# A four-layer graph network: bias and row transfers re-queued, one scatter moved to the next block, the first embedding product moved, and one-hots of 128 rows in place of 35

## The chip, the core and the metric

The kernel runs on one core of a Trainium2 chip. The metric is the device time of one execution in microseconds; the time before is the median of three executions. The engines are called PE (TensorE, the matrix unit), DVE (VectorE), ACT (ScalarE), POOL (GpSimd) and SP (SyncE, which here only issues transfers).

## The reference

`x` holds 625 nodes of 768 features. Each of four stages is `x = x + layer(relu(layernorm(x)))`. What the layers compute, cut to the core:

```python
# L0: mean over the edges of each of 34 relations, one weight per relation
h1 = jnp.einsum('rni,rio->no', mean, W_rel) + x @ W_root + b_rgcn      # called "relations" below
out = gcn(h1, W_gcn) + b_gcn                                           # l0b
# L1: two gcn layers
h = relu(gcn(h, W1) + b1);  out = gcn(h, W2) + b2                      # l1a, l1b
# L2: the node's type embedding (3 types, 128 numbers) is joined to the features
h = jnp.concatenate([x, node_emb[node_type]], axis=-1)                 # 768 + 128 = 896
h = relu(rgcn_conv(h, ..., w_rel1, w_root1, b1))                       # l21, 3 kinds of edge, 896 -> 896
h = relu(rgcn_conv(h, ..., w_rel2, w_root2, b2))                       # l22
h = relu(rgcn_conv(h, ..., w_rel3, w_root3, b3))                       # l23
# L3: one gcn layer                                                    # l3
```

## The kernel before

The nodes lie in 5 tiles of 125 rows (`NP`, `NT`), the features in chunks of 128 (`fc` of them: 6 for width 768, 7 for 896). Float32 products are done as three products of rounded parts, hi by hi, hi by lo and lo by hi; ACT makes the high part of a chunk (`w_high`) and DVE subtracts it for the low part (`w_low`). The program has three parts that follow one another, with all engines meeting between them.

**The prepare block** (0 to 137.8 us). SP issues, in its queue's order: the edge lists, the ten pieces of `x`, a broadcast of the bias of the first layer into the DRAM tensor `sums` (L1309), the root weight `root_w` (L1310), a fill of spare rows (L1312) and, when the normalised rows are there, two stores of them to `rows` (L1316). PE turns the rows (L1668), ACT copies the turned chunks to `root_g` (L1400, L1401), and then PE takes turns of root products (L1684; `root(6)` first, which waits for `root_w`) and of slot counts (L1694), for which DVE builds comparison tables in five chunks (L1526 to L1533), two buffers deep, so that chunk 2 waits for the first `slots`. At the end the root products of node tiles 0 to 4 come from PE, ACT copies them into `h` (`take`), and POOL adds tile `d` to `sums` by an indirect DMA (L1367) for d = 0 to 3; the one of tile 4 is POOL's first transfer in the next block (L2100). These adds wait for the bias.

**`add_means`** (to 851.6 us). Thirty-three units of relation weights: POOL gathers rows of `rows` into `e_raw` (L2064), SP loads the list `list_now` and weights, ACT and DVE split them, PE multiplies, and POOL scatters the result onto `sums` (L2076). At its end ACT issues eight transfers that bring `sums` back to `h` in four parts of columns (`ROW_PARTS`, L2212); the next block's engines wait for each part by `loaded[i]`.

**`layers`** (from 854 us). All other layers, with one stream of weight chunks: SP loads chunk n into `w_raw`, a ring of 4 (L377), once DVE has taken chunk n - 4. Ahead of the first sums PE runs `AWAKE` times two products on nothing of use (L1019). The sums over edges are L821 and the products with weights L871; product tile k goes to one of two banks `ps_o`, and DVE's `take` (L602) adds it to `x`.

For `l21` the seventh chunk of the features is the embedding, and it is not stored per node: each node has a one-hot of its type, 35 columns wide (`HOT`: the three types at columns 0 to 2 and again at 32 to 34), and per kind of edge `typed_rows` (L843) multiplies the embedding with the seventh weight chunk into 35 rows, which ACT (L452) and DVE (L644, subtraction for the lower copy) put into `w_lo` as `typed`. Product tiles then have one pair of matmuls of 35 rows for this chunk in place of three pairs of 128. `w.order` of these weights begins with chunk 6, so it is loaded first. `turn` (L906) turns a tile of rows, the last chunk with 35 columns; ACT copies 750 columns (L477) and the 35 x 125 piece (L478).

## Time and profile before

| what | value |
|---|---|
| time, median of 3 runs | 1698.94 us (1697.83 to 1699.77) |
| the profiled execution | 1708.87 us, span 1707.2 us, granted clock 0.970 |
| PE / weight loads / DVE / ACT / POOL busy | 95% / 88% / 57% / 37% / 20% |
| data moved | 227.53 MB, 133 GB/s over the span |
| prepare block, last instruction of ACT ends | 137.8 us |
| relation weights end, ACT's last issue | 851.6 us |

The span is that of the instructions on the core; the profiled execution's time is 1.7 us more. The profiled execution is 9.9 us longer than the median of the runs without a profile. In the rows below a line is that of the kernel before, "[6.61 <-PE ...]" is the time that the engine sat idle before the row and what ended it, and "x34" counts instructions of one kind that the row stands for. PEclk is the clock that TensorE was granted, 1.00 being 2.4 GHz and 0.50 being 1.2 GHz.

### The profile page before, as it was taken

What the parts mean: (1) busy time and instruction counts of PE and PEld (TensorE: products, weight loads), DVE (VectorE), ACT (ScalarE), POOL (GpSimd) and SP (SyncE); (2) the same over time, 40 slices, a digit from 0 to 9 for tenths busy, and PEclk for the clock granted to TensorE, in tenths of its full rate; (3) what the DMA queues carried; (4) which work ended last, traced back from release to release, by engine and by line L of the source; (5) the groups of instructions that cost most, each with busy time, mean ns of one, the idle gap of its engine ahead of it and who ended that gap; (6) DMA issues with size and microseconds to landing.
All of it is one profiled execution on the core that took longest, in us unless ns stands there. A gap on an engine that the chain in (4) does not pass through costs nothing. (4 is left out here: it accounts for less than half of the span.)

```text
span 1707.2 us, 28150 instructions
## 1 busy us (share of the span) xinstructions
PE 1628.4 (95%) x9954; PEld 1498.6 (88%) x9955; DVE 981.2 (57%) x1486; ACT 626.3 (37%) x858; POOL 333.3 (20%) x297
## 2 busy tenths in 40 slices
PE   6998998999999999999799989999999999999997
PEld 4766887999999998888699988899899999999997
DVE  7784885786766678555376573255252442523372
ACT  6113564555555565555143223112231222312230
POOL 1203544453443343442110000000010000000000
PEclk8869999999999999999899999999999999999999
DMA  6225897687997799996442130231122112221101
GB/s 221 44 69 139 243 261 196 190 253 206 253 263 202 203 270 247 266 263 173 74 122 65 52 114 24 72 92 36 56 66 84 56 57 83 58 73 56 56 28 46
DMA packets 96605, 227.53 MB, mean 133 GB/s; under 512 B 11987, under 2 KB 36326, under 8 KB 96524
## 3 DMA queue, kind: packets, MB, share of 16 engines
q1 hardware_dynamic: 68471, 150.07, 27.6%
q0 software_dynamic: 21552, 71.98, 18.7%
q10 hardware_dynamic: 6501, 4.33, 1.0%
q8 instruction: 60, 0.98, 0.2%
q14 instruction: 21, 0.17, 0.0%
HBM read 186.94 MB, written 41.29 MB: 134 GB/s over the span
## 5 line engine op out<-in xcount | busy, mean ns | idle before, releaser
L871 PE MATMUL layers_ps_o<-layers_w_lo,layers_g_hi 128*125 128x384 f32 (+2 forms) x900 | 239.4, 347 | 4.6 <-DVE layers_w_lo L644 4.6
L2513 PE MATMUL l_means_ps<-l_means_w_hi,l_means_g_hi 128*128 128x512 f32 (+1 forms) x912 | 238.3, 342 | 3.6 <-DVE l_means_g_lo L2373 3.6
L2147 ACT CAST l_means_w_hi<-w_raw 128x768 fp32r<-128x768 f32 x204 | 170.2, 838 | 190.2 <-PE l_means_ps L2513 186.7
L2362 DVE TENSOR_TENSOR l_means_w_lo<-w_raw,l_means_w_hi 128x768 fp32r<-128x768 f32 x204 | 186.6, 948 | 89.2 <-ACT l_means_w_hi L2147 89.0
L2513 PE MATMUL l_means_ps<-l_means_w_hi,l_means_g_lo 128*128 128x512 f32 (+1 forms) x912 | 235.5, 339 | 0.0
L2513 PE MATMUL l_means_ps<-l_means_w_lo,l_means_g_hi 128*128 128x512 f32 (+1 forms) x912 | 234.0, 338 | 0.0
L871 PE MATMUL layers_ps_o<-layers_w_hi,layers_g_hi 128*125 128x384 f32 (+1 forms) x870 | 230.5, 346 | 0.8 <-DVE layers_w_lo L584 0.8
L871 PE MATMUL layers_ps_o<-layers_w_hi,layers_g_lo 128*125 128x384 f32 (+1 forms) x870 | 228.6, 344 | 0.0
L2497 PE MATMUL l_means_ps<-pick,e_hi 128*128 128x256 f32 (+1 forms) x612 | 167.7, 304 | 18.8 <-issue 18.3
L655 DVE TENSOR_TENSOR h_lo<-layers_ps_o,h_hi 125x768 fp32r<-125x768 f32 (+1 forms) x45 | 45.1, 1002 | 237.8 <-ACT h_hi L484 237.8
L871 PEld LDWEIGHTS layers_ps_o<-layers_w_lo,layers_g_hi 128*125 128x125 f32 (+1 forms) x900 | 162.7, 186 | 12.4 <-DVE layers_w_lo L644 4.9
L2513 PEld LDWEIGHTS l_means_ps<-l_means_w_hi,l_means_g_hi 128*128 128x128 f32 x912 | 152.5, 189 | 22.7 <-issue 2.9
L2513 PEld LDWEIGHTS l_means_ps<-l_means_w_lo,l_means_g_hi 128*128 128x128 f32 x912 | 153.8, 189 | 20.9
L2513 PEld LDWEIGHTS l_means_ps<-l_means_w_hi,l_means_g_lo 128*128 128x128 f32 x912 | 154.1, 188 | 19.1
L2076 POOL DMA_INDIRECT sums<-l_means_y,l_means_row_now x76 | 129.2, 1700 | 206.7 <-ACT l_means_y L2182 176.9
L2497 PE MATMUL l_means_ps<-pick,e_lo 128*128 128x256 f32 (+1 forms) x612 | 165.6, 300 | 0.0
L871 PEld LDWEIGHTS layers_ps_o<-layers_w_hi,layers_g_hi 128*125 128x125 f32 x870 | 156.5, 186 | 8.5 <-issue 3.4
L871 PEld LDWEIGHTS layers_ps_o<-layers_w_hi,layers_g_lo 128*125 128x125 f32 x870 | 158.2, 186 | 3.5
L2373 DVE TENSOR_TENSOR l_means_g_lo<-l_means_ps,l_means_g_hi 128x512 fp32r<-128x512 f32 (+1 forms) x126 | 78.3, 637 | 125.8 <-ACT l_means_g_hi L2161 124.8
L821 PE MATMUL layers_ps_g<-a,h_hi 125*128 125x316 f32 x590 | 136.0, 312 | 7.1 <-DVE h_lo L626 2.5
L2497 PEld LDWEIGHTS l_means_ps<-pick,e_hi 128*128 128x128 f32 x612 | 119.7, 196 | 22.1 <-issue 19.8
L2064 POOL DMA_INDIRECT e_raw<-rows,l_means_src_now x99 | 127.0, 1283 | 49.5 <-POOL l_means_src_now L2061 27.2
(363 smaller groups left out, 2405.6 us busy)
## 6 DMA issues: line engine op xcount, KB each, us to landing
w_raw<-in_L_gnn_W_rel SPq DMA_DIRECT2D x204, 384.0 KB, 6.8
layers_w_raw<-in_L_gnn_w_rel SPq DMA_DIRECT2D x39, 384.0 KB, 7.8
layers_w_raw<-in_L_gnn_w_rel SPq DMA_DIRECT2D x21, 448.0 KB, 8.3
layers_a_raw<-adj SPq DMA_DIRECT2D x9, 769.0 KB
layers_w_raw<-in_L_gnn_W SPq DMA_DIRECT2D x18, 384.0 KB, 3.5
list_now<-targets SPq DMA_DIRECT2D x33, 192.0 KB
layers_w_raw<-in_L_gnn_w_root SPq DMA_DIRECT2D x13, 384.0 KB, 3.4
layers_w_raw<-in_L_gnn_w_root SPq DMA_DIRECT2D x7, 448.0 KB, 4.5
```

Of the source, the lines that this page charges most:

```text
L655: v.tensor_tensor(in_halves(h_lo[:, k, 0:layer.width]), out_rows(bank, layer.width), in_halves(h_hi[:, k, 0:layer.width]).bitcast(F32), AL ...
L821: mm = t.matmul(to[:, at:at + PART[p]], rows[:, k, f * 128:(f + 1) * 128], a[:, k, cols], start=(k == 0 and i == 0), stop=(k == NT - 1 and ...
L871: mm = t.matmul(ps_o[0:NP, i % 2, a_half, 0:half], g, part_of_w[:, a_half * half:(a_half + 1) * half], start=(f == order[0] and n == 0), s ...
L2064: nc.gpsimd.indirect_dma_start(out=e_raw[:, j, :], out_offset=None, in_=rows, in_offset=bass.IndirectOffsetOnAxis(ap=src_now[:, j:j + 1], ...
L2076: nc.gpsimd.indirect_dma_start(out=sums, in_=y[:, j, :], in_offset=None, compute_op=ALU.add, out_offset=bass.IndirectOffsetOnAxis(ap=row_n ...
L2147: nc.scalar.copy(w_hi[:, f, :], w_raw[:, f, :]).then_inc(w_hi_ready, 1)
L2362: v.tensor_tensor(w_lo[:, f, :], w_raw[:, f, :], w_hi[:, f, :].bitcast(F32), ALU.subtract)\
L2373: v.tensor_tensor(g_lo[:, f:f + per, at], sums_in_bank(f // per, tiles), g_hi[:, f:f + per, at].bitcast(F32), ALU.subtract).then_inc(g_rea ...
L2497: mm = t.matmul(sums, e[:, j, f * 128:(f + 1) * 128], pick[:, j, 0:cols], start=(j == 0 and part == 0), stop=(j == UNIT - 1 and part == 1))
L2513: mm = t.matmul(ps_y[j][:, o0:o1], g[:, f, at], w[:, f, o0:o1], start=(f == 0 and opens and g is g_hi and w is w_hi), stop=(f == fc - 1 an ...
```

## The change

- SP issues the bias broadcast behind the two stores of rows, so `root_w` follows `x` at once. `WARM_ROWS`, a count of products without use ahead of the turns, goes from 16 to 32.
- The scatter of root tile 3 leaves the prepare block and is issued by POOL in the next one, ahead of that of tile 4.
- Of the eight transfers that bring `sums` back, ACT issues two (part 0) before the blocks meet, and SP six at the start of the last block, ahead of the bias and of the first weights. `AWAKE` goes from 8 to 6.
- `typed_rows` of the first kind of `l21` moves on PE from ahead of that layer to behind product tile 0 of `l1b`. ACT and DVE split chunk 6 of its weight, and build `typed`, correspondingly earlier. The other two kinds stay.
- The one-hots are 128 columns wide (zeros from column 35), so that the pair of matmuls of the embedding has 128 rows; the turned chunk is copied together with the other six.

The diff, cut to what the prediction speaks of:

```diff
+def fetch_rows(engine, source, h, i, loaded):
+    at = slice(ROW_PARTS[i][0] * 128, ROW_PARTS[i][1] * 128)
+    rows = source.rearrange("(k p) f -> p k f", p=NP)
+    for part in (slice(0, 112), slice(112, NP)):
+        engine.dma_start(h[part, :, at], rows[part, :, at]).then_inc(loaded[i], 16)
...
+    @block.sync
+    def _(sp):
+        for i in range(1, len(ROW_PARTS)):
+            fetch_rows(sp, source, h, i, loaded)
...
-AWAKE = 8
+AWAKE = 6
...
-            nc.scalar.copy(tile_columns(g_hi, k, fc - 1), turned_tile(k, fc - 1)).then_inc(layer.g_hi_ready, 1)
-            nc.scalar.copy(g_hi[0:HOT, fc - 1, column(k):column(k) + NP], ps_g[0:HOT, k % 2, (fc - 1) * 128:(fc - 1) * 128 + NP])\
-                .then_inc(layer.g_hi_ready, 1)
+            nc.scalar.copy(tile_columns(g_hi, k, fc), turned_tile(k, fc)).then_inc(layer.g_hi_ready, 1)
...
         summed_high(l1b)
+        w_high(l21.w[0], 0)
+        typed_rows_high(l21.w[0])
         root_of(l1b, 0)
...
+        dve.wait_ge(emb_high, 1)
+        v.tensor_tensor(emb_parts[1], part[:, 0:HOT], emb_parts[0].bitcast(F32), ALU.subtract).then_inc(emb_ready, 1)
         summed_low(l1b)
+        w_low(l21.w[0], 0)
         add_bias(l1b)
...
             take(l1b, k)
+            if k == 1:
+                typed_rows_low(l21.w[0])
...
-                    terms = ((g_hi[0:HOT, f, at], typed),)
+                    terms = ((g_hi[:, f, at], w_lo[:, f, :]),)
...
-        gcn_products(l1b, range(NT - 1))
+        gcn_products(l1b, (0,))
+        pe.wait_ge(emb_ready, 1)
+        typed_rows(l21.w[0])
+        gcn_products(l1b, range(1, NT - 1))
+        pe.wait_ge(typed_ready, 1)
         turn(0)
...
-            sp.dma_start(sums, bias.unsqueeze(0).broadcast_to([N, width])).then_inc(bias_stored, 16)
             sp.dma_start(root_w[:], w_root.rearrange("(f p) o -> p f o", p=128)).then_inc(root_loaded, 16)
...
+            sp.dma_start(sums, bias.unsqueeze(0).broadcast_to([N, width])).then_inc(bias_stored, 16)
             sp.wait_ge(nodes_used, tiles // group)
...
-            for d in range(NT - 1):
+            for d in range(NT - 2):
...
+            for d in (NT - 2, NT - 1):
+                nc.gpsimd.indirect_dma_start(out=sums, in_=second.h[:, d, 0:width], in_offset=None, compute_op=ALU.add,
+                                             out_offset=bass.IndirectOffsetOnAxis(ap=node_rows[:, d:d + 1], axis=0))\
+                    .then_inc(root_added, 16)
```

What the change does to the order of instructions is shown at three places. First SP's queue in the prepare block, before, from the last two pieces of `x` to the first relation weights:

```order
L1308 DMA x_rows<-in_x 112x768
L1308 DMA x_rows<-in_x 13x768
L1309 DMA sums<-in_L_gnn_b_rgcn 625x768
L1310 DMA prep_root_w<-in_L_gnn_W_root 128x6x768
L1312 DMA sums<-prep_empty_rows 2304x1x128
L1316 DMA rows<-h_rows 112x5x768
L1316 DMA rows<-h_rows 13x5x768
L1319 DMA w_raw<-in_L_gnn_W_rel 128x768 x6
```

The same place of the change:

```order
L1327 DMA x_rows<-in_x 112x768
L1327 DMA x_rows<-in_x 13x768
L1328 DMA prep_root_w<-in_L_gnn_W_root 128x6x768
L1330 DMA sums<-prep_empty_rows 2304x1x128
L1334 DMA rows<-h_rows 112x5x768
L1334 DMA rows<-h_rows 13x5x768
L1335 DMA sums<-in_L_gnn_b_rgcn 625x768
L1338 DMA w_raw<-in_L_gnn_W_rel 128x768 x6
```

The bias broadcast moved past three transfers and now stands last ahead of the relation weights.

Second DVE at the start of `l1b`'s products, before: the last pair of splits of `l1b` (w_lo, g_lo), the bias for five tiles, and the takes of tiles 0 and 1:

```order
L584 TENSOR_TENSOR layers_w_lo<-layers_w_raw,layers_w_hi 128x768
L591 TENSOR_TENSOR layers_g_lo<-layers_ps_g,layers_g_hi 128x630
L597 TENSOR_TENSOR x_rows<-x_rows,layers_bias_rows 125x768 x5
L602 SCALAR_TENSOR_TENSOR x_rows<-layers_ps_o,dinv,x_rows 125x768
L88 BN_STATS layers_stats<-x_rows 125x6 x2
L602 SCALAR_TENSOR_TENSOR x_rows<-layers_ps_o,dinv,x_rows 125x768
L88 BN_STATS layers_stats<-x_rows 125x6 x2
```

And of the change (L601 is the old L584, L614 the old L597, L619 the old L602):

```order
L601 TENSOR_TENSOR layers_w_lo<-layers_w_raw,layers_w_hi 128x768
L608 TENSOR_TENSOR layers_g_lo<-layers_ps_g,layers_g_hi 128x630
L601 TENSOR_TENSOR layers_w_lo<-layers_w_raw,layers_w_hi 128x896
L614 TENSOR_TENSOR x_rows<-x_rows,layers_bias_rows 125x768 x5
L619 SCALAR_TENSOR_TENSOR x_rows<-layers_ps_o,dinv,x_rows 125x768
L88 BN_STATS layers_stats<-x_rows 125x6 x2
L619 SCALAR_TENSOR_TENSOR x_rows<-layers_ps_o,dinv,x_rows 125x768
L661 TENSOR_TENSOR layers_w_lo<-layers_ps_g,layers_w_lo 3x896
L88 BN_STATS layers_stats<-x_rows 125x6 x2
```

The split of `l21`'s first weight chunk (128x896) came ahead of the bias and of every take, and the subtraction for `typed` behind the take of tile 1.

Third PE at the end of `l1b`'s last product tile, before: the three pairs of `typed_rows` (L843), and the first pair of `l21`:

```order
L871 MATMUL layers_ps_o<-layers_w_hi,layers_g_hi 125x384 x2
L871 MATMUL layers_ps_o<-layers_w_lo,layers_g_hi 125x384 x2
L871 MATMUL layers_ps_o<-layers_w_hi,layers_g_lo 125x384 x2
L843 MATMUL layers_ps_g<-layers_w_hi,layers_g_lo 35x448 x2
L843 MATMUL layers_ps_g<-layers_w_lo,layers_g_lo 35x448 x2
L843 MATMUL layers_ps_g<-layers_w_hi,layers_g_lo 35x448 x2
L871 MATMUL layers_ps_o<-layers_w_hi,layers_g_hi 125x448 x2
```

And of the change, where they stand now, between product tiles 0 and 1 of `l1b` (L863 is the old L843, L891 the old L871):

```order
L891 MATMUL layers_ps_o<-layers_w_hi,layers_g_hi 125x384 x2
L891 MATMUL layers_ps_o<-layers_w_lo,layers_g_hi 125x384 x2
L891 MATMUL layers_ps_o<-layers_w_hi,layers_g_lo 125x384 x2
L863 MATMUL layers_ps_g<-layers_w_hi,layers_g_lo 35x448 x2
L863 MATMUL layers_ps_g<-layers_w_lo,layers_g_lo 35x448 x2
L863 MATMUL layers_ps_g<-layers_w_hi,layers_g_lo 35x448 x2
L891 MATMUL layers_ps_o<-layers_w_hi,layers_g_hi 125x384 x2
```

The three pairs moved ahead of four of the five product tiles of `l1b`.

## Rows read from the trace of the kernel before

**Rows 1.** The page: busy time of TensorE, its share and count

```profile
PE 1628.4 (95%) x9954; PEld 1498.6 (88%) x9955; DVE 981.2 (57%) x1486; ACT 626.3 (37%) x858; POOL 333.3 (20%) x297
```

**Rows 2.** Timeline of PE, 27 to 66 us (start, duration, operation, idle before)

```profile
27.12 1.40 PE L1668 MATMUL prep_ps<-ident,h_rows 125*128 125x125 f32 x10 [0.21 <-ACT prep_root_g L1401]
34.40 6.89 PE L1684 MATMUL prep_ps<-prep_root_w,prep_root_g 128*125 128x384 f32 x12 [5.88 <-DMA prep_root_w<-in_L_gnn_W_root]
41.13 2.91 PE L1694 MATMUL prep_ps<-prep_is_tile,w_raw 125*128 125x186 f16 x34
...
65.29 4.06 PE L1684 MATMUL prep_ps<-prep_root_w,prep_root_g 128*125 128x384 f32 x12
```

**Rows 3.** Timeline of DVE in the prepare block: tables of chunk 2; index build

```profile
44.08 1.29 DVE L1526 TENSOR_TENSOR prep_is_slot<-prep_iota,prep_slot_of 125x2176 f16<-125x2176 f16 x1 [6.61 <-PE prep_ps L1694]
...
65.49 0.35 DVE L1547 TENSOR_SCALAR s_src_index<-prep_ps 128x186 int32<-128x186 f32 x1 [4.74 <-PE prep_ps L1694]
```

**Rows 4.** Timeline of ACT in the prepare block, its last turned copy

```profile
29.03 0.27 ACT L1401 COPY prep_root_g<-prep_ps 128x125 f32<-128x125 f32 x1
```

**Rows 5.** Table by stretches: engines' busy time, PEclk, DMA share, GB/s

```profile
16.00:20.00 4.00, 2.46 (x12) 0.91 (x10) 3.31 (x12) 2.69 (x7) 0.00 (x0) 1.00 0.95 346
27.00:35.00 8.00, 2.00 (x11) 1.54 (x12) 7.89 (x7) 5.12 (x8) 0.00 (x0) 0.89 0.34 123
141.00:143.00 2.00, 0.00 (x0) 0.00 (x0) 0.00 (x0) 0.59 (x1) 0.00 (x0) 0.85 0.00 0
979.00:986.00 7.00, 7.00 (x42) 7.00 (x41) 5.99 (x8) 0.00 (x0) 0.00 (x0) 1.00 0.99 250
```

**Rows 6.** Timeline of ACT at the two block changes; last, of POOL's root scatters

```profile
142.41 1.28 ACT L2139 ACT_TABLE_LOAD   x1 [4.60 <-PEq L64]
...
847.79 3.83 ACTq L2212 DMA_DIRECT2D h_rows<-sums  x8
854.13 0.72 ACT L134 CAST a<-adj_all 125x630 fp32r<-125x630 uint16 x1 [15.71 <-PEq L64]
...
130.36 1.99 POOL L1367 DMA_INDIRECT sums<-h_rows,node_rows  x1 [29.55 <-ACT h_rows L1409]
...
DMA to landing us min/median/max: 10.0/10.6/13.9
```

**Rows 7.** Timeline of ACT and DVE in the first unit of relation weights

```profile
158.87 0.84 ACT L2143 CAST e_hi<-e_raw 128x768 fp32r<-128x768 f32 x1 [0.15 <-DMA e_raw<-rows,l_means_src_now]
...
159.97 1.07 DVE L2351 TENSOR_SCALAR pick<-list_now,s_slot_dst 128x384 fp32r<-128x384 f32 x3 [5.55 <-DMA list_now<-targets]
```

**Rows 8.** Timeline of ACT; then the page's list of DMA issues (landing)

```profile
865.45 0.84 ACT L448 CAST layers_w_hi<-layers_w_raw 128x768 fp32r<-128x768 f32 x1
...
layers_w_raw<-in_L_gnn_W_gcn SPq DMA_DIRECT2D x6, 384.0 KB, 10.7
```

**Rows 9.** Timeline of DVE, ACT and PE, 978 to 1037 us

```profile
978.53 4.42 DVE L597 TENSOR_TENSOR x_rows<-x_rows,layers_bias_rows 125x768 f32<-125x768 f32 x5
983.52 1.02 DVE L602 SCALAR_TENSOR_TENSOR x_rows<-layers_ps_o,dinv,x_rows 125x768 f32<-125x768 f32 x1 [0.56 <-PE layers_ps_o L871]
...
1013.26 0.94 ACT L448 CAST layers_w_hi<-layers_w_raw 128x896 fp32r<-128x896 f32 x1 [3.76 <-DMA layers_w_raw<-in_L_gnn_w_rel]
...
1025.08 1.10 PE L871 MATMUL layers_ps_o<-layers_w_lo,layers_g_hi 35*125 35x448 f32 x2 [4.56 <-DVE layers_w_lo L644]
...
1036.16 0.67 PE L871 MATMUL layers_ps_o<-layers_w_lo,layers_g_hi 35*125 35x448 f32 x2
```

**Rows 10.** Timeline of PE in kind 1; then its groups by form

```profile
1146.60 0.57 PE L871 MATMUL layers_ps_o<-layers_w_hi,layers_g_hi 128*125 128x448 f32 x2
...
1148.22 0.56 PE L871 MATMUL layers_ps_o<-layers_w_lo,layers_g_hi 128*125 128x448 f32 x2
...
1150.23 0.56 PE L871 MATMUL layers_ps_o<-layers_w_lo,layers_g_hi 128*125 128x448 f32 x2
...
L871 PE MATMUL layers_ps_o<-layers_w_lo,layers_g_hi 35*125 35x448 f32 x30 | 10.5, 430 | 4.6 <-DVE layers_w_lo L644 4.6
```

More of the change, by code:

```diff
@@ L102, in row_scales, with load_rows @@
     newton_rsqrt(v, then, rstd[:, at], var[:, at], tmp[:, at])
-def load_rows(nc, block, sem, loaded, h, parts, dinv, adj_all, a, a_parts, a_ready, buffers):
+ROW_PARTS = ((0, 1), (1, 2), (2, 4), (4, 6))
+def fetch_rows(engine, source, h, i, loaded):
[3 more added lines that the diff above has]
+        engine.dma_start(h[part, :, at], rows[part, :, at]).then_inc(loaded[i], 16)
+def load_rows(nc, block, sem, source, loaded, h, parts, dinv, adj_all, a, a_parts, a_ready, buffers):
     fc = ROW_PARTS[-1][-1]
@@ L500, in kind_step @@
             w = after(layer.w[r])
-            if layer is l21:
+            if layer is l21 and r > 0:
                 typed_rows_high(layer.w[r])
@@ L553, in _ @@
         root_of(l1b, 2)
-        for f in range(l21.w[0].fc):
+        for f in range(1, l21.w[0].fc):
             w_high(l21.w[0], f)
@@ L646, in turned_low @@
         def turned_low(layer, k):
-            dve.wait_ge(layer.g_hi_ready, 2 * k + 2)
+            dve.wait_ge(layer.g_hi_ready, k + 1)
             fc = layer.w[0].fc - 1
@@ L687, in kind_products @@
         def kind_products(layer, r):
-            if layer is l21:
+            if layer is l21 and r > 0:
                 typed_rows_low(layer.w[r])
@@ L767, in _ @@
             if k == NT - 1:
-                dve.wait_ge(emb_high, 1)
-                v.tensor_tensor(emb_parts[1], part[:, 0:HOT], emb_parts[0].bitcast(F32), ALU.subtract).then_inc(emb_ready, 1)
                 turned_low(l21, 1)
-                for f in range(l21.w[0].fc):
+                for f in range(1, l21.w[0].fc):
                     w_low(l21.w[0], f)
             take(l1b, k)
+            if k == 1:
+                typed_rows_low(l21.w[0])
             then(row_statistics(v, stats, x, k))
@@ L904, in turn @@
             for f in range(l21.w[0].fc):
-                size = HOT if f == l21.w[0].fc - 1 else 128
-                mm = t.transpose(ps_g[0:size, k % 2, f * 128:f * 128 + NP], h[:, k, f * 128:f * 128 + size], ident[0:NP, 0:NP])
+                mm = t.transpose(ps_g[:, k % 2, f * 128:f * 128 + NP], h[:, k, f * 128:(f + 1) * 128], ident[0:NP, 0:NP])
             mm.then_inc(l21.turned, 1)
         def kind_products(layer, r):
-            if layer is l21:
-                if r == 0:
-                    pe.wait_ge(emb_ready, 1)
-                    pe.wait_ge(layer.g_ready, 1)
-                else:
-                    pe.wait_ge(layer.e_taken, place_of(layer, r, 0) - 1)
+            if layer is l21 and r > 0:
+                pe.wait_ge(layer.e_taken, place_of(layer, r, 0) - 1)
                 typed_rows(layer.w[r])
@@ L962, in root_columns @@
                     if by_type and f == w.fc - 1:
-                        terms = ((typed[:, out_chunk], g_hi[0:HOT, f, :]),)
+                        terms = ((w_lo[:, f, out_chunk], g_hi[:, f, :]),)
                     else:
@@ L1066 @@
 WARM = 16
-WARM_ROWS = 16
+WARM_ROWS = 32
 def by_runs(rows, run):
@@ L1815 @@
 Background = namedtuple("Background", "src dst etype kinds adj adj_all ident h node_types emb rows_loaded")
-ROW_PARTS = ((0, 1), (1, 2), (2, 4), (4, 6))
 def add_means(nc, tag, units, w_rel, rows, sums, plan, src_index, slot_dst, row_index, row_inv, targets, node_rows, list_rows,
@@ L2099, in _ @@
             nc.gpsimd.nop().then_inc(index_ready, 1)
-            nc.gpsimd.indirect_dma_start(out=sums, in_=second.h[:, NT - 1, 0:width], in_offset=None, compute_op=ALU.add,
-                                         out_offset=bass.IndirectOffsetOnAxis(ap=node_rows[:, NT - 1:NT], axis=0))\
-                .then_inc(root_added, 16)
+            for d in (NT - 2, NT - 1):
+                nc.gpsimd.indirect_dma_start(out=sums, in_=second.h[:, d, 0:width], in_offset=None, compute_op=ALU.add,
+                                             out_offset=bass.IndirectOffsetOnAxis(ap=node_rows[:, d:d + 1], axis=0))\
+                    .then_inc(root_added, 16)
             iota(key_iota[:], [[1, keys]])
@@ L2207, in _ @@
             act.wait_ge(all_added, 1)
-            to = second.h
-            summed_rows = sums[0:N, :].rearrange("(k p) f -> p k f", p=NP)
-            for i, (f0, f1) in enumerate(ROW_PARTS):
-                for part in (slice(0, 112), slice(112, NP)):
-                    nc.scalar.dma_start(to[part, :, f0 * 128:f1 * 128], summed_rows[part, :, f0 * 128:f1 * 128])\
-                        .then_inc(second.rows_loaded[i], 16)
+            fetch_rows(nc.scalar, sums[0:N, :], second.h, 0, second.rows_loaded)
         @block.vector
@@ L2299, in embeddings @@
                 then(ins)
-                then(v.memset(second.h[:, :, width:width + HOT], 0.0))
+                then(v.memset(second.h[:, :, width:width + 128], 0.0))
                 for at in (0, 32):
@@ L2605, in gnn_kernel @@
         a_parts = sem("a_parts")
-        loaded = load_rows(nc, block, sem, rows_loaded, h, parts, dinv, adj_all, a, a_parts, a_ready, buffers)
+        loaded = load_rows(nc, block, sem, sums0[0:N, :], rows_loaded, h, parts, dinv, adj_all, a, a_parts, a_ready, buffers)
         layers(nc, block, sem, buffers, loaded, x, h, acc, parts, a, a_parts, a_ready, adj_all, adj2, inv_dram, dinv, ident, d, out)
```

## Prediction

> **What bounds the kernel now.** I read the page first: TensorE is busy 95% of the span and no other engine over 57% [rows 1], so time can only go where PE idles, runs at the lower clock, or does work that it could do faster. Next I took PE's timeline and looked for "idle before" over 0.3 us, and for the same operation with two durations. Four places lie under this change. In the prepare block PE idles 5.88 us until `root_w` has landed, and its first twelve root products then take 6.73 us (34.40 to 41.13) where twelve take 4.06 later [rows 2]; DVE, whose table for chunk 2 waits for the slots behind these products, idles 6.61 us with them [rows 3]. At the change of blocks ACT idles 4.60 us the first time, and the second time from the end of its issues (847.79 + 3.83 = 851.62) to 854.13, 2.51 us [rows 6]. In `l21` PE waits 4.56 us for `typed` [rows 9]. And in each product tile of `l21` the pair of matmuls with 35 rows stands in a wider gap than the others [rows 10].
>
> **Bias behind the rows.** Before, the bias broadcast goes ahead of `root_w`. The reader should see that from 27 to 35 us, while PE waits, the transfer engines are only 34% busy and move 123 GB/s, where 16 to 20 us show 95% and 346 GB/s [rows 5]: what runs there is slow, not queued behind much else. Without it `root_w` (2304 KB) takes 2304/346 = 6.8 us once `x` is through. Lower bound of its landing: `x` is in by about 10 us, hence 17 us. Upper: only the slow stretch goes, 34.4 - 8 = 26.4 us. Both are ahead of the last turned copy of ACT, which ends at 29.03 + 0.27 = 29.30 [rows 4], and on which the same products wait. So they start at 29.3, 5.1 us earlier. The doubled warm-up products should leave the clock at 2.4 GHz, so the twelve take 4.0 us, not 6.73; slots of chunk 0 then stand at 33.3 and not at 41.13, and end 2.8 us later at 36.1. From there DVE decides: it is free at 44.08 - 6.61 = 37.47 [rows 3] and needs about 5.57 us for each of chunks 2 to 4 (an even beat that PE's rounds follow), so the last table is there at 54.2 and the last slots end at 57.2, where before the next root products began at 65.29 [rows 2]. Term: **-8.0**. If the clock stays low for the twelve, slots 0 end at 38.8, chunk 2 starts 5.3 earlier, and the term is -5.3. Behind this point everything waits for PE: DVE's index build sat idle 4.74 us for the last slots [rows 3]. The bias itself lands by about 45 us, ahead of the first scatter-add; its cover is some 18 us, and gone it would cost what it exceeds.
>
> **Root tile 3 moved.** Its scatter is issued at 130.36 and the median of its kind lands 10.6 us later, at 141.0 [rows 6]; from 141 to 143 us nothing moves [rows 5], and ACT goes on at 142.41, 1.4 us behind the landing. The second block change, with no scatter of that kind at its end, takes 2.5 us, not 4.6. I read this as the blocks meeting only when that transfer is done: **-2.1**; if they don't wait for it, 0. In the next block POOL issues one scatter more ahead of the three gathers of the first unit, 1.99 us and 0.3 between [rows 6]. The gathers' last split on ACT ends at 158.87 + 0.84 = 159.71, but DVE, held by `list_now` until 159.97, needs the third split only after three `pick` (1.0) and two `e_lo` (1.8), at about 162.8 [rows 7]. The cover is 3.0 us and hides the 2.3: **0**.
>
> **Rows brought back.** ACT issues 2 transfers, not 8, so its 3.83 us become 1.0 and the last block begins 2.9 us sooner [rows 6]. But the six others now are SP's, 0.48 us each and ahead of bias and weights, so `W_gcn` is asked for at the same moment as before, about 854.4. It landed 10.7 us later, at 865.1, and ACT took it at 865.45 [rows 8]: a slack of 0.35. The early start is thus lost on the weight. If the landing does not move, the term is -0.35; if the 2.9 us by which the rows' transfers shift go wholly onto it, it is 865.1 + 2.9 - 865.45 = +2.6. It has the rows' traffic right ahead of it now, so I take the middle: **+1.0**. Six `AWAKE` rounds for eight save nothing, since PE waits for rows behind them.
>
> **First embedding product.** Gains: the wait for `typed` of 4.56 us [rows 9]. Behind it PE works at the lower clock: the 35-row pair there takes 1.10 us and the same pair a tile later 0.67; in that proportion over the pair, the turn and the next three pairs it is 2.3 us. ACT waited 3.76 us at 1013.26 for the fifth weight chunk, whose place in the ring comes free only when chunk 0 is split; with that split some 20 us earlier this wait goes; PE, whose 18 pairs ahead of the 1025.08 row need 7.3 us at 0.405, had about 1.6 of it. Together -8.4. Cost: the products need weight chunk 6, which is asked for behind a transfer of edge counts. From 979 to 986 the transfer engines are 99% busy at 250 GB/s [rows 5], 448 KB taking 1.8 us; the chunk lands between 981 and 986, and I take 985, since four chunks share that stretch. High part 0.94, a low part hardly longer and the hand-overs give 987.1. PE ends tile 0 at 983.5, as the take of tile 0 shows [rows 9], so it stalls 3.6 us, and the clock falls as above but with nothing but full pairs behind, 1.3 us; hand-over of `typed` 0.5. Behind that wait on DVE stand the bias adds (982.95 - 978.53 = 4.42) and the takes: take 0 ends at 992.5, while PE wants its bank for tile 2 only at 994, so no second stall. Term: -8.4 + 5.4 = **-3.0**; -8.0 if the chunk lands by 981.4, and 0 if at 988.
>
> **128 rows.** Four starts of pairs without a 35-row one span 1148.22 - 1146.60 = 1.62 us, and four with one 1150.23 - 1148.22 = 2.01 [rows 10], so such a pair costs 0.39 more than one of 128 rows. There are 15 (x30 in pairs), and one in each of the 7 chunks of the root product: 22 x 0.39 = 8.6. Three of them lie where PE waits anyway: **-7.4**; bounds 0 and -8.6. The one copy of 875 columns for 750 and 125, the wider zeros and the wider turn stand beside PE's products, 0.
>
> The row says that 35 rows are slower. The Trainium skill, "TensorE: Matmul & The Clock Gate", section "Why this matters for your kernels", has a single matmul of 32 rows take the same time as one of 128. By that rule this term would be 0 and the sum -12.1; the trace does not agree, with 2.01 for 1.62 us, unless the gap comes from something else that stays.
>
> **Sum**: -8.0 - 2.1 + 1.0 - 3.0 - 7.4 = -19.5. The profiled execution takes 1708.9 us, so 1689.4 with a profile; it stands 9.9 us above the median of the plain runs, and the same off that median, 1698.9 - 19.5, gives **1679.5 us**.
>
> **Rivals.**
> - *The first weight chunk of `l21` is early*, by 981.4: the stall in `l1b` is gone, 1674.5. For it, the engines are free for other queues while the counts load; against, 99% busy until 986. 0.12.
> - *Rows in a matmul cost nothing* and the gap has another cause (the change doesn't do what it says there): 1679.5 + 7.4 = 1686.9. 0.09.
> - *Two scatters hold up the gathers.* Landings of this kind run from 10.0 to 13.9 us [rows 6], the longer ones where two follow closely. If the gathers come 3.9 us later beside the 2.3, 6.2 - 3.0 = +3.2: 1682.7; with twice that delay 1686.6. 0.14.
> - *Weights late at both waits*: `W_gcn` by the whole 2.9 (+1.6 on my term) and chunk 6 at 988 (+3): 1684.1. 0.11.
> - *Slower than before*: the stall ahead of the embedding product costs PE its clock for long. `l1b`'s four tiles behind it have 18 pairs each, 0.35 us apart, 25 us in all, and take twice that at 1.2 GHz. It outweighs the other terms and the 0.2% once the clock is down for some 22 us. Against: behind 4.56 us of idleness the pair times are normal again within 5 us, after 5.88 us within about 7 [rows 2, 9]. At worst 1679.5 + 25 = 1704. 0.02.
>
> **How the numbers follow.** My forecast, 1675.5 to 1683.5 with the bounds of single terms, has 0.52. The range takes in the early chunk in part, the rule of rows and the scatters: 1673 to 1687. A difference under 0.2% (3.4 us) can't be told from none here; faster than that means under 1695.5, which all cases but the last reach: faster 0.96, within 0.02, slower 0.02.
>
> **What the new profile should show.** The first L1684 row at about 29.3 without a wait for `root_w`, and the last slots ending near 57. ACT's idle time at the first block change near 2.5 us, and e_hi not waited for by DVE. ACT's first high part of `W_gcn` at about 856.3 (865.45 less 10.1, plus 1.0), waiting for the transfer. A PE row at the embedding product with 3 to 4 us of idleness, and none for `typed` in `l21`. Pairs of the seventh chunk 0.405 us apart like the rest. I am wrong if DVE's table of chunk 2 starts later than 39, if the gathers of the first unit make PE wait, or if PE idles more than 5 us behind tile 0 of `l1b`.

## The result

The change makes the kernel 0.5% faster: the ratio of its time to that of before is 0.9947, with a 95% interval of 0.9928 to 0.9967 (nine runs each, medians 1692.14 and 1703.21 us). On the 1698.94 us shown ahead of the prediction that is about 9 us, to 1689.9; the forecast was 19.5, and 1689.9 lies above both of its ranges (to 1683.5, and to 1687 with the rivals). The two profiled executions differ by 8.6 us in their span (1707.2 and 1698.6).

The page of the changed kernel; TensorE is as busy as before, to be read with [rows 1], and a DMA that brings rows back now stands in the chain that ended last:

```profile
PE 1621.6 (95%) x9966; PEld 1499.9 (88%) x9967; DVE 981.5 (58%) x1486; ACT 625.3 (37%) x853; POOL 334.7 (20%) x297
...
PE 42%; DVE 5%; DMA 2%; ACT 1%; issue 0%; SPq 0%; DVEq 0%
PE layers_ps_o L891 25%; PE layers_ps_g L841 9%; PE layers_ps_g L985 4%; PE layers_ps_g L1017 3%; DMA layers_w_raw<-in_L_gnn_w_rel 1%; DVE layers_w_lo L601 1%; DMA h_rows<-sums 1%; DVE h_lo L643 0%; DVE layers_stats L88 0%; ACT h_hi L488 0%; ACT layers_w_hi L465 0%; DVE x_rows L619 0%; DVE layers_part L688 0%; PE layers_ps_g L863 0%; DMA layers_w_raw<-in_L_gnn_w_root 0%
```

A single total does not say which part did what, because one stretch of the kernel takes a different time in each trace. So I divide each trace at instructions that all kernels have, and give the time from one of these cuts to the next. All cuts are starts of rows of the timelines of ACT and DVE, but for the end of ACT's last take.

| from ... to ... | before | after | difference | forecast |
|---|---|---|---|---|
| start to the end of ACT's last take of the prepare block | 137.81 | 129.32 | -8.49 | -8.0 |
| to ACT's first instruction of `add_means` | 4.60 | 1.15 | -3.45 | -2.1 |
| to the first low part of 512 columns in the first unit | 33.11 | 35.19 | +2.08 | 0 |
| to ACT's first transfer of rows (32 units) | 672.27 | 673.82 | +1.55 | 0 |
| to ACT's first instruction of the last block | 6.34 | 6.34 | 0 | -2.9 |
| to the first high part of `W_gcn` | 11.32 | 17.27 | +5.95 | +3.9 |
| to `l0b`'s take of tile 0 | 18.15 | 20.45 | +2.30 | 0 |
| to `l1b`'s take of tile 0 | 99.92 | 109.42 | +9.50 | } -3.0 |
| to the low part of `l21`'s second product | 54.29 | 44.89 | -9.40 | } |
| to the last take | 660.66 | 652.04 | -8.62 | -7.4 |

The differences sum to -8.58. The gain of the prepare block is lost almost to the microsecond at the second change of blocks (+8.25 in three rows), where +1.0 was forecast.

PE in the prepare block, to be read with [rows 2]: no wait for `root_w` is left, the twelve root products start at 28.67 and take 4.11 us (6.89 before), and the last ones start at 57.17 where they started at 65.29.

```profile
28.67 4.11 PE L1703 MATMUL prep_ps<-prep_root_w,prep_root_g 128*125 128x384 f32 x12 [0.92 <-ACT prep_root_g L1420]
32.61 2.91 PE L1713 MATMUL prep_ps<-prep_is_tile,w_raw 125*128 125x186 f16 x34
...
57.17 4.06 PE L1703 MATMUL prep_ps<-prep_root_w,prep_root_g 128*125 128x384 f32 x12
```

ACT at the two block changes, to be read with [rows 6]: the first idle time is 1.15 us, not 4.60. At the second, the issues take 1.21 us and not 3.83, but the time from their start to the next block (845.82 - 839.48) is 6.34 us, exactly as before (854.13 - 847.79).

```profile
130.47 1.28 ACT L2158 ACT_TABLE_LOAD   x1 [1.15 <-PEq L64]
...
839.48 1.21 ACTq L114 DMA_DIRECT2D h_rows<-sums  x2
845.82 0.72 ACT L151 CAST a<-adj_all 125x630 fp32r<-125x630 uint16 x1 [16.49 <-PEq L64]
...
863.09 0.83 ACT L465 CAST layers_w_hi<-layers_w_raw 128x768 fp32r<-128x768 f32 x1
```

DVE in the last block: before, its row multiplications (L158) waited for no transfer, as in these two rows of the kernel before:

```profile
856.58 0.83 DVE L158 TENSOR_TENSOR h_rows<-h_rows,dinv 125x640 f32<-125x640 f32 x1
...
859.62 0.82 DVE L158 TENSOR_TENSOR h_rows<-h_rows,dinv 125x640 f32<-125x640 f32 x1
```

Now (L175) they wait three times, 7.45 us in all. The weight `W_gcn` is not waited for in this trace: ACT's row at 863.09 above has no idle time before it.

```profile
849.33 0.83 DVE L175 TENSOR_TENSOR h_rows<-h_rows,dinv 125x640 f32<-125x640 f32 x1 [2.66 <-DMA h_rows<-sums]
...
853.70 0.83 DVE L175 TENSOR_TENSOR h_rows<-h_rows,dinv 125x640 f32<-125x640 f32 x1 [2.81 <-DMA h_rows<-sums]
...
858.72 0.82 DVE L175 TENSOR_TENSOR h_rows<-h_rows,dinv 125x640 f32<-125x640 f32 x1 [1.98 <-DMA h_rows<-sums]
```

And around the moved embedding product, to be read with [rows 9]: ACT gets the weight chunk at 986.52, PE has waited 5.35 us for its low part, its pairs are then 0.73 to 0.75 us apart, and the take of tile 0, at 983.52 before, is at 992.96.

```profile
986.52 0.94 ACT L465 CAST layers_w_hi<-layers_w_raw 128x896 fp32r<-128x896 f32 x1 [8.78 <-DMA layers_w_raw<-in_L_gnn_w_rel]
...
988.72 0.93 PE L863 MATMUL layers_ps_g<-layers_w_hi,layers_g_lo 128*35 128x448 f32 x2 [5.35 <-DVE layers_w_lo L601]
989.45 0.95 PE L863 MATMUL layers_ps_g<-layers_w_lo,layers_g_lo 128*35 128x448 f32 x2
...
992.96 1.02 DVE L619 SCALAR_TENSOR_TENSOR x_rows<-layers_ps_o,dinv,x_rows 125x768 f32<-125x768 f32 x1
```

### The profile page after: what moved, and what is told of

It reads as the page before. It is cut to its first block, busy times and chain, and to the rows that moved or that the text cites. A ratio compares the mean times of both kernels' runs of the same rounds, so it can differ in the third digit from the quotient of the medians.

```text
span 1698.6 us, 28171 instructions
## 1 busy us (share of the span) xinstructions
PE 1621.6 (95%) x9966; PEld 1499.9 (88%) x9967; DVE 981.5 (58%) x1486; ACT 625.3 (37%) x853; POOL 334.7 (20%) x297
## 4 chain that ended last, share of the span: by engine, by line
PE 42%; DVE 5%; DMA 2%; ACT 1%; issue 0%; SPq 0%; DVEq 0%
PE layers_ps_o L891 25%; PE layers_ps_g L841 9%; PE layers_ps_g L985 4%; PE layers_ps_g L1017 3%; DMA layers_w_raw<-in_L_gnn_w_rel 1%; DVE layers_w_lo L601 1%; DMA h_rows<-sums 1%; DVE h_lo L643 0%; DVE layers_stats L88 0%; ACT h_hi L488 0%; ACT layers_w_hi L465 0%; DVE x_rows L619 0%; DVE layers_part L688 0%; PE layers_ps_g L863 0%; DMA layers_w_raw<-in_L_gnn_w_root 0%
## 5 line engine op out<-in xcount | busy, mean ns | idle before, releaser
L891 PE MATMUL layers_ps_o<-layers_w_lo,layers_g_hi 128*125 128x384 f32 (+1 forms) x900 | 237.6, 345 | 0.0
L891 PE MATMUL layers_ps_o<-layers_w_hi,layers_g_hi 128*125 128x384 f32 (+1 forms) x870 | 229.7, 345 | 0.8 <-DVE layers_w_lo L601 0.7
L891 PE MATMUL layers_ps_o<-layers_w_hi,layers_g_lo 128*125 128x384 f32 (+1 forms) x870 | 228.6, 344 | 0.0
L891 PEld LDWEIGHTS layers_ps_o<-layers_w_lo,layers_g_hi 128*125 128x125 f32 x900 | 163.9, 186 | 3.9
L891 PEld LDWEIGHTS layers_ps_o<-layers_w_hi,layers_g_hi 128*125 128x125 f32 x870 | 157.4, 186 | 6.1 <-DVE layers_w_lo L601 1.4
L891 PEld LDWEIGHTS layers_ps_o<-layers_w_hi,layers_g_lo 128*125 128x125 f32 x870 | 158.2, 186 | 3.4
```

What stands on the lines that cost most here:

```text
L891: mm = t.matmul(ps_o[0:NP, i % 2, a_half, 0:half], g, part_of_w[:, a_half * half:(a_half + 1) * half], start=(f == order[0] and n == 0), s ...
```

## The experiments

**Each part alone.** First the row fetch, alone on the kernel before (`AWAKE` goes with it):

```diff
+        for i in range(1, len(ROW_PARTS)):
+            fetch_rows(sp, source, h, i, loaded)
...
-            for i, (f0, f1) in enumerate(ROW_PARTS):
+            fetch_rows(nc.scalar, sums[0:N, :], second.h, 0, second.rows_loaded)
```

> The kernel before with the row fetch alone changed. Theory: the last block does not start sooner when ACT issues two transfers in place of eight, because in both traces it starts 6.34 us after ACT's first issue; parts 1 to 3 are therefore only asked for at its start, DVE waits for them and PE's clock falls: the first high part of W_gcn comes about 6 us later against ACT's first issue, and the take of tile 0 of l0b about 8 us later (891.8 for 883.6), so about 8 us slower in all. Rival (the term of my prediction): the block starts 2.9 us sooner and only the weight's landing costs, +1.0 us in all.

Measured: ratio 1.0068 (1.0042 to 1.0094), slower. From ACT's first transfer to the block 6.34 us; to the first high part of `W_gcn` 16.74 us for 11.32; from there to the take 18.16, as before. So +5.4 us in the trace and +8.25 in that of the changed kernel. The mechanism stands: the block does not start sooner, and the rival's -2.9 is not there.

The plain runs lose more than this stretch of the trace: 0.42 to 0.94% are 7 to 16 us. The profiled execution, 1705.8 us, is the fastest of the ten; the granted clock of the ten is 0.967 on the mean, that of the kernel before 0.971. Where the rest is lost was not traced. The effect of `AWAKE` was not tested apart.

Of the 2.8 us between the two traces, 0.5 lie ahead of the high part of `W_gcn` (17.27 and 16.74), and 2.3 behind it. These 2.3 are a matter of TensorE's clock, which two groups of rows show. PE's first sum behind the wait for DVE in this kernel:

```profile
864.94 0.55 PE L838 MATMUL layers_ps_g<-a,h_hi 125*128 125x316 f32 x2 [2.37 <-DVE layers_g_lo L608]
865.33 0.46 PE L838 MATMUL layers_ps_g<-a,h_lo 125*128 125x316 f32 x2
865.62 0.47 PE L838 MATMUL layers_ps_g<-a,h_hi 125*128 125x316 f32 x2
```

and in the changed kernel:

```profile
865.69 0.89 PE L841 MATMUL layers_ps_g<-a,h_hi 125*128 125x316 f32 x2 [4.26 <-DVE layers_g_lo L608]
866.38 0.73 PE L841 MATMUL layers_ps_g<-a,h_lo 125*128 125x316 f32 x2
866.90 0.73 PE L841 MATMUL layers_ps_g<-a,h_hi 125*128 125x316 f32 x2
```

After 2.37 us of idleness the pairs behind the first are 0.29 us apart, at 2.4 GHz; after 4.26 us they are 0.52 to 0.53 apart, at 1.2 GHz, for 5 us, and ten steps, each 0.15 to 0.30 us longer, make the 2.3. The table of stretches has the granted clock of both from 866 to 870 us, first the changed kernel, then the other:

```profile
866.00:870.00 4.00, 4.00 (x16) 4.00 (x16) 3.68 (x5) 1.87 (x3) 0.00 (x0) 0.50 0.75 204
```

```profile
866.00:870.00 4.00, 4.00 (x29) 4.00 (x28) 4.00 (x6) 2.54 (x4) 0.00 (x0) 1.00 0.81 225
```

Then the one-hots of 128 rows alone:

```diff
-                    terms = ((g_hi[0:HOT, f, at], typed),)
+                    terms = ((g_hi[:, f, at], w_lo[:, f, :]),)
```

> The kernel before with one-hots of 128 rows alone. Theory: the pair of matmuls with 35 rows costs 0.39 us more than one with 128, 22 times, so -8.6 us, all of it between the third tile of l21's first kind and the end of l22's start; everything ahead of l21 stays within 0.1 us. Rival (row count does not matter, the gap is something else): 0, and what the changed kernel gained there comes from the moved embedding product (-8.6 then shows only together with it).

Measured: from `l0b`'s first take to the last take 806.34 us, 814.87 before: -8.5 us, in the place expected. Over all traces that stretch is at 815.1 us on the mean in the six kernels that have the old one-hots and the old place of the embedding product (814.28 to 816.04), and `row_sizes` below, with 128 and 96 rows, has 806.33 too: -8.7. The ratio, 0.9974 (0.9945 to 1.0003), says less than this (below). The rival is out.

The first embedding product alone:

```diff
-        gcn_products(l1b, range(NT - 1))
+        gcn_products(l1b, (0,))
+        pe.wait_ge(emb_ready, 1)
+        typed_rows(l21.w[0])
+        gcn_products(l1b, range(1, NT - 1))
```

> The kernel before with the first embedding product alone moved. Theory: PE stalls 5.2 to 5.4 us behind tile 0 of l1b for the weight chunk that lands at about 986.5, the clock falls, take 0 is 9.4 us later, and by the second tile of l21 all of it is given back by the wait for the typed rows that is gone: 0.0 to +0.2 us in all. Rival (my prediction): -3.0 us, since the ring of weight chunks runs ahead.

Measured: ratio 1.0001 (0.9974 to 1.0027). From `l0b`'s first take to `l1b`'s 109.47 us for 99.92, and from there to `l21`'s second product 44.27 for 54.29: -0.5 in all, which is 0 within the 2 us by which this stretch varies. So it is as the theory said, and not -3.0.

The bias behind the rows alone, with 32 warm-up products:

```diff
-            sp.dma_start(sums, bias.unsqueeze(0).broadcast_to([N, width])).then_inc(bias_stored, 16)
...
+            sp.dma_start(sums, bias.unsqueeze(0).broadcast_to([N, width])).then_inc(bias_stored, 16)
-WARM_ROWS = 16
+WARM_ROWS = 32
```

> The kernel before with the bias broadcast behind the rows and 32 warm-up products, nothing else. Theory: ACT's last take of the prepare block ends 8.5 us sooner, and as the rest of the kernel waits for nothing that is bound to the clock on the wall, the whole kernel is 8 us shorter. Rival: the scatter of root tile 3, still in this block, keeps its distance to the last take, so the gain stays, but the first unit's gathers or the relation loop lose part of it again: 4 to 6 us.

Measured: ACT's last take ends at 129.90 us, 7.9 sooner than in the trace of before. Over all traces of this study it is at 136.6 on the mean with the old prepare block (nine kernels, 135.64 to 137.81) and at 129.8 with the new one (four, 129.32 to 130.14), so the edit is worth 6.8 us, and the trace of before was a late one. The ratio is 0.9980 (0.9956 to 1.0004), about half of what the stage gained, and can't tell theory from rival. Which of the two edits did it, the order of the transfers or the 32 products, was not tested apart. Why the ratios are blurred can be seen in the traces: the 32 units of relation weights (fourth row of the table) took 661.3 to 674.3 us over the thirteen kernels, one trace each, all with the same instructions in that loop; the four traces of one and the same chip have 661.3, 664.5, 671.4 and 674.3. A part worth 8 us is within that spread. Each of the other stretches repeats within about 2.2 us among the kernels that have the same code there, and those from ACT's first transfer of rows to `l1b`'s take within 0.1, but for one of 0.3.

The scatter of root tile 3 alone:

```diff
-            for d in range(NT - 1):
+            for d in range(NT - 2):
...
+            for d in (NT - 2, NT - 1):
```

> The kernel before with the scatter of root tile 3 alone moved. Theory: the change of blocks takes 1.2 us in place of 4.6 to 4.8, and the first unit takes 1.5 to 2 us longer from its first instruction to the first low part of its second stage (35.2 for 33.1 to 33.5), since its list of targets and the gathers come later: -1.5 to -2 us together. Rival: the first unit keeps its 33.3 us, and the whole 3.5 stays.

Measured, in the one execution of this kernel: 1.15 us at the change of blocks and 35.63 us in the first unit. The nine kernels without this edit have 4.44 to 4.80 there (mean 4.64) and 33.11 to 34.90 (mean 33.77), so it is -3.5 and +1.9: -1.6 us together. What the 4.6 us were is settled by the landing of the scatter of root tile 3: in each of the nine kernels ACT goes on 1.47 us behind it (before: issued at 130.36, landed 10.58 us later at 140.94, ACT at 142.41), though the landing itself moves from 133.2 to 140.9 us. In the changed kernel the loss can be seen on DVE and ACT, to be read with [rows 7]:

```profile
150.57 1.08 DVE L2365 TENSOR_SCALAR pick<-list_now,s_slot_dst 128x384 fp32r<-128x384 f32 x3 [8.72 <-DMA list_now<-targets]
```

```profile
150.90 0.84 ACT L2162 CAST e_hi<-e_raw 128x768 fp32r<-128x768 f32 x1 [1.83 <-DMA e_raw<-rows,l_means_src_now]
```

DVE waits 8.72 us for the list, 5.55 before, and ACT 1.83 for the third gather, 0.15 before. Counted from the start of the block, the third gather's split starts 4.0 us later than before (20.4 for 16.5). The third split ends at 151.74, before DVE wants it at about 153.4; the list, a plain transfer of SP's, came 20.1 us after the start of the block and not 17.6, and DVE's rows put it ahead of the gathers in setting the time. Had the list been on time, the gathers would have cost about 0.9 us (an estimate: DVE would have wanted the third split at 150.8, 2.5 us sooner). Why it is later beside one scatter more is open.

**The change without the row fetch.** If the account holds, taking back one of five parts must nearly double the gain.

```diff
-            fetch_rows(nc.scalar, sums[0:N, :], second.h, 0, second.rows_loaded)
+            for i, (f0, f1) in enumerate(ROW_PARTS):
-AWAKE = 6
+AWAKE = 8
```

> The changed kernel with the row fetch and AWAKE put back to what they were. Theory (the row fetch lost 8.25 us of 17.7 gained): from ACT's first row issue to the take of tile 0 of l0b 29.5 us, as before, not 37.7; the whole kernel about 8 us faster than the change and 17 faster than before, ratio 0.990. Rival (what the first block gains is lost behind the second change of blocks in any case, for instance on the weights of l0b): that stretch stays above 33 us and the ratio near 0.994.

Measured: ratio 0.9902 (0.9869 to 0.9934), median 1684.34 us. ACT's rows, to be read with those of the change above:

```profile
837.91 3.83 ACTq L2215 DMA_DIRECT2D h_rows<-sums  x8
844.25 0.72 ACT L134 CAST a<-adj_all 125x630 fp32r<-125x630 uint16 x1 [15.75 <-PEq L64]
...
855.57 0.83 ACT L448 CAST layers_w_hi<-layers_w_raw 128x768 fp32r<-128x768 f32 x1
```

ACT is at its issues for 3.83 us, the block starts 6.34 us after the first of them, as in the other kernels, and the high part of `W_gcn` comes 11.32 us later; the take of `l0b` stands 35.82 us behind the first transfer, 44.06 in the changed kernel. (The 29.5 and 37.7 of the expectation are counted from the start of the block and not from the first transfer, 6.34 us less: 29.48 measured.) The rival is out: the gain of the first block is not lost here in any case.

**The embedding product one tile later**, on top of that:

```diff
-        gcn_products(l1b, (0,))
+        gcn_products(l1b, (0, 1))
...
-        w_low(l21.w[0], 0)
         add_bias(l1b)
...
-            if k == 1:
+            if k == 2:
                 typed_rows_low(l21.w[0])
             then(row_statistics(v, stats, x, k))
+            if k == 0:
+                w_low(l21.w[0], 0)
```

> As the run without the row fetch, and the first embedding product one tile later: on PE behind product tile 1 of l1b, on DVE the split of the weight behind the statistics of tile 0 and that of the typed rows behind the take of tile 2. Theory: chunk 6 lands at 986.5 and PE is busy with tile 1 until 989.9, so PE does not stall and the clock stays up; from l0b's first take to l1b's first 99.9 us, not 109.4, and in all 6 to 8 us faster than the run beside it, ratio to before 0.986. Rival: the time goes into the wait for the later weight chunks of l21 instead (three waits on ACT for their landing), and at the second product tile of l21 less than 2 us are left of it.

Measured: ratio 0.9858 (0.9829 to 0.9888), median 1677.51 us, the fastest kernel of this study. PE around the product shows neither a wait nor the lower clock:

```profile
982.84 0.51 PE L875 MATMUL layers_ps_o<-layers_w_hi,layers_g_lo 128*125 128x384 f32 x2
983.19 0.57 PE L847 MATMUL layers_ps_g<-layers_w_hi,layers_g_lo 128*35 128x448 f32 x2
...
984.41 0.51 PE L875 MATMUL layers_ps_o<-layers_w_hi,layers_g_hi 128*125 128x384 f32 x2
```

From `l0b`'s first take to `l21`'s second product it takes 147.03 us; in the changed kernel it is 154.31, in the run beside it 154.99, and in the two kernels with the same one-hots and the product in its old place (`onehots_only`, `row_sizes`) 153.63 and 153.25. So the move is worth 6 to 7 us when PE does not have to wait for it, and nothing here, where it waited 5.35 us and went on at the lower clock.

**Which row counts cost.** The pair of matmuls of the embedding with 128, 64 and 96 rows:

```diff
-                    terms = ((g_hi[:, f, at], w_lo[:, f, :]),)
+                    rows = (128, 64, 96, 128)[typed_number(w)]
+                    terms = ((g_hi[0:rows, f, at], w_lo[0:rows, f, :]),)
```

> The kernel before with one-hots of 128 rows, but the pair of matmuls of the embedding with 128 rows in l21's first kind, 64 in the second and 96 in the third (the rows left out are zeros). Theory (a change of the number of row groups that a matmul uses costs): the pair of 64 and that of 96 cost about 0.39 us more than one of 128, as 35 did. Rival (only a number of rows that is not a multiple of 32 costs): 64 and 96 cost nothing more. Second rival (the cost grows with the rows missing): 64 costs more than 96, and both less than 0.39.

Measured, in the groups by form (count, busy, mean ns of one):

```profile
L870 PE MATMUL layers_ps_o<-layers_w_lo,layers_g_hi 96*125 96x448 f32 x10 | 2.9, 369 | 0.0
```

The mean of 369 ns is that of the full pairs (the pairs of 35 rows had 430, [rows 10]), and the pairs are 0.41 us apart like their neighbours: 96 rows cost as much as 128. The number 64 had gone to the root weights, which use another line, so no kind ran with it; hence a second kernel with `(128, 128, 64, 65)`:

> As row_sizes, where 96 rows cost nothing (pairs 0.41 us apart as their neighbours) and the 64 fell on no kind: now 64 rows in the second kind and 65 in the third. Theory formed from that run: a matmul of at most 64 rows, coming between matmuls of 125 or 128, costs the 0.39 us per pair, one of more than 64 nothing; 64 shows 1.21 to 1.23 us for the two pairs behind the one ahead in place of 0.8, 65 shows none. Rival: only 32 rows or partial row groups cost, so both 64 and 65 cost nothing, or 65 costs and 64 does not.

Measured:

```profile
L870 PE MATMUL layers_ps_o<-layers_w_lo,layers_g_hi 64*125 64x448 f32 x10 | 3.4, 414 | 0.0
L870 PE MATMUL layers_ps_o<-layers_w_lo,layers_g_hi 65*125 65x448 f32 x10 | 2.9, 369 | 0.0
L870 PEld LDWEIGHTS layers_ps_o<-layers_w_lo,layers_g_hi 64*125 64x125 f32 x10 | 1.4, 182 | 1.4 <-issue 1.4
L870 PEld LDWEIGHTS layers_ps_o<-layers_w_lo,layers_g_hi 65*125 65x125 f32 x10 | 1.8, 187 | 0.1
```

And a pair of 64 rows among its neighbours:

```profile
1136.83 0.56 PE L870 MATMUL layers_ps_o<-layers_w_hi,layers_g_lo 128*125 128x448 f32 x2
1137.32 0.67 PE L870 MATMUL layers_ps_o<-layers_w_lo,layers_g_hi 64*125 64x448 f32 x2
1137.92 0.68 PE L870 MATMUL layers_ps_o<-layers_w_hi,layers_g_hi 128*125 128x448 f32 x2
1138.43 0.56 PE L870 MATMUL layers_ps_o<-layers_w_lo,layers_g_hi 128*125 128x448 f32 x2
```

From 1136.83 to 1138.43 these are 1.60 us where three steps of full pairs take 1.21; a pair of 65 at 1201.44 has its neighbours at 1201.04, 1201.85 and 1202.26, 1.22 us. So of the five numbers tried, 35 and 64 rows cost 0.39 us a pair, and 65, 96 and 128 nothing more; the step lies between 64 and 65. Numbers between 35 and 64, or below 35, were not run. From `l0b`'s first take to the last take this kernel has 810.09 us, 3.8 more than with 96 and 128 rows; its five pairs of 64 account for 2.0, and the rest is within what the stretch varies by. The weight loads show where the time lies: ahead of the ten loads of 64 rows the engine stood idle 1.4 us, ahead of those of 65 rows 0.1. That a load of few rows can't be made beside a running matmul of many would explain it; it is a guess, not shown.

**What starts the last block.** Two kernels, one execution each. POOL's part, on the kernel before; the memsets write a buffer that is read no more:

```diff
             nc.gpsimd.nop().then_inc(all_added, 1)
+            for j in range(3):
+                nc.gpsimd.memset(y[:, j, :], 0.0)
```

> The kernel before with three memsets of 128 x 768 on POOL behind the instruction that releases ACT's row fetch (they write a buffer that nothing reads any more). Six of six kernels start the last block 6.34 us after ACT's first row issue, with two or with eight issues. Theory: POOL sets that time, so the block starts later by the whole duration of the three memsets. Rival: another engine or a fixed time sets it, and it stays 6.34.

Measured, on POOL and ACT:

```profile
836.88 2.09 POOL L2137 MEMSET l_means_y<- 128x768 f32 x3 [5.51 <-DMA sums<-l_means_y,l_means_row_now]
...
836.80 3.83 ACTq L2214 DMA_DIRECT2D h_rows<-sums  x8
845.29 0.72 ACT L134 CAST a<-adj_all 125x630 fp32r<-125x630 uint16 x1 [18.28 <-PEq L64]
```

The memsets take 2.09 us, and the block starts 8.49 us after ACT's first transfer, 2.15 later than in the other kernels. Then ACT's part, sixteen transfers of half the columns for eight:

```diff
+                    for half in range(2):
+                        cols = slice((f0 + f1) * 64 - (1 - half) * (f1 - f0) * 64, (f0 + f1) * 64 + half * (f1 - f0) * 64)
+                        nc.scalar.dma_start(to[part, :, cols], summed_rows[part, :, cols])\
```

> The kernel before with the eight row transfers of ACT cut into sixteen of half the columns. Theory: ACT's issues take about 7.7 us and now decide: the last block starts 1 to 2.5 us behind the last of them, 9 to 10 us after the first. Rival: the start stays at 6.34 us, independent of ACT.

```profile
841.54 7.83 ACTq L2214 DMA_DIRECT2D h_rows<-sums  x16
850.69 0.72 ACT L134 CAST a<-adj_all 125x630 fp32r<-125x630 uint16 x1 [18.88 <-PEq L64]
```

ACT is at it until 849.37 and the block starts 1.32 us later, 9.15 after the first. So the meeting took 1.32 us behind ACT when ACT came last here, and 1.15 us at the first change of blocks with no scatter outstanding. At this place ACT came last in this kernel alone. In the others it is POOL: lengthening its work by 2.09 us moved the start by 2.15, and the block starts 6.32 us behind the end of the memsets, so POOL is ready only about 5 us after its last instruction (an estimate, 6.32 less 1.3). What POOL does in that time, whether it closes its queue of indirect transfers or something else, is open.

## Why the prediction was wrong

- **"ACT issues 2 transfers, not 8 ... and the last block begins 2.9 us sooner" is the step that failed.** I took ACT for the last to arrive because its 2.51 us of idleness behind its issues looked like the price of a meeting, and set it beside the 4.60 of the first change as the time of a meeting without a transfer outstanding. The meeting costs 1.15 to 1.32 us; the other 1.2 us of the 2.51 were a wait for POOL, and POOL does not get faster. So nothing is gained, and the transfers of parts 1 to 3, which before ran during that dead time, are asked for 5 us later. I had costed their lateness on `W_gcn` alone, which in the changed kernel is not waited for at all (0.77 us in the kernel with the row fetch alone). What was late were the rows themselves: DVE waits 7.45 us for them, and behind it PE's sums and its clock. The term was +1.0, with +2.6 as its bound; it is +8.25 in the changed kernel and +5.4 alone.
- **Bias behind the rows.** Forecast -8.0, measured -8.5 in this pair of traces and -6.8 on the means of all. The chain was as told: the products wait for ACT's last turned copy (28.67 against 29.3), and the next root products follow the last slots at 57.17, as forecast with 57.2.
- **Root tile 3.** "The blocks meeting only when that transfer is done" holds (1.47 us from landing to ACT in nine kernels), and is worth more than forecast, -3.45 for -2.1, for the reason above: I compared with a change of blocks that was itself held up by POOL. "The cover hides the 2.3: 0" does not hold; the first unit lost 2.1 us, as `list_now` landed later, which I had left at its old place. The two errors nearly cancel: -1.4 in this pair and -1.6 alone, for -2.1.
- **First embedding product.** The mechanism was right and two sizes off. The chunk came at 986.5 for 985, so PE stood 5.35 us and not 3.6, past the 5 us that I had named as a sign of being wrong; and the pairs behind ran at the lower clock for longer. 9.5 us were lost at `l1b`'s first take where about 6.6 were forecast (5.4, and the 1.2 that the product itself takes there now). Nearly all of it, 9.4, came back in `l21`, where 9.6 were forecast (8.4, and the 1.2 that moved). The term is +0.1 for -3.0 (0 to +1 without the two pairs of the one-hots that gained in the same stretch), just past the bound of 0 that I gave for a landing at 988, though the chunk was there by 986.5: the bound had the clock too cheap. Its way to be a gain, one tile later, was not in my prediction.
- **128 rows.** Forecast -7.4, measured -8.6 in the last row of the table and, alone, -8.5 to -8.7; for all 22 pairs -8.6 was my bound, so also the pairs that I thought to lie in PE's waits counted. Two of the 22 lie ahead of the last cut, so some 0.8 of the gain stands in the row above, and the -8.6 of the last row has 0.8 of luck in it: on the means of all traces that stretch went from 660.3 to 652.6, -7.7. It was right to go by the row. The Trainium skill, "TensorE: Matmul & The Clock Gate", section "Why this matters for your kernels", has a single matmul of 32 rows take the time of one of 128; carried over to this stream of matmuls, that does not hold: 35 and 64 rows cost 0.39 us more a pair.
- **The rivals.** None of them was what happened. "Two scatters hold up the gathers" had the right stretch: the third gather came 4.0 us later, but it was the late list that set the time, and the stretch lost 2.1 us and not 3.2 or more. "Weights late at both waits" came nearest, with the right places; it gave 1684.1, and the ratio puts the change at 1698.94 x 0.9947 = 1689.9.

With the terms as measured, -8.5 - 1.4 + 8.25 + 0.1 - 8.6 = -10.1, and +1.55 from the relation units, which vary by 13 us with the same code: -8.6, the difference of the two spans. The parts alone, by their traces, are +5.4, -8.5, -0.5, -6.8 and -1.6, -12.0 in all. The plain runs fit less well: the four ratios of the parts multiply to 1.002, and the change has 0.995. The row fetch loses some 6 us more by its ratio than by its trace, and the one-hots and the bias gain some 4 and 3 us less, these two within their intervals. The loss of the row fetch beyond its trace stays open.

## What to carry to other kernels

When all engines meet, ask for each of them when it arrives, and read it from two meetings: a shorter list on one engine gains nothing while another is later, and it may have been what filled the dead time. A product that is moved ahead pays only if its operand has landed when the engine gets there: here one tile later turned 0 into 6 to 7 us. And where a stage of the kernel varies by 13 us from trace to trace, divide the trace at common instructions and compare stretch by stretch before believing a total.

## What the runs showed of the hardware

- In a stream of matmuls with 128 rows (448 columns), a pair with 35 or 64 rows cost 0.39 us more, and one with 65, 96 or 128 nothing.
- TensorE after 2.37 us of idleness went on at 2.4 GHz; after 4.26 us and after 5.35 us it was granted 1.2 GHz, for about 5 us in both.
- A meeting of all engines took 1.15 to 1.32 us behind the last to arrive. With an indirect transfer of POOL's outstanding it took 4.4 to 4.8 us behind ACT, which was 1.47 us behind the landing of that transfer in all nine kernels, and at the end of the relation units 6.34 us from ACT's first transfer, which POOL releases, the same to 0.01 us in eleven kernels, with two or with eight issues on ACT.
- In the last 8 us ahead of the landing of `root_w` the transfer engines had been 34% busy [rows 5]; with the bias broadcast behind the rows, no engine waits for `root_w` or for the bias.
